# A fourth buffer of normalised tiles, absolute values moved up in ScalarE's order, and a group's moments taken over three pieces of rows

## What is computed

```python
x = x + _L0_conv_ref(_gn(x), ...)   # shifted-window attention, 7x7 windows, 8 heads
x = x + _L1_conv_ref(_gn(x), ...)   # 3x3 convolution of signs, scaled by a box sum of |x|
x = x + _L2_conv_ref(_gn(x), ...)   # 3x3 convolution with the signs of the kernel
x = x + _L3_conv_ref(_gn(x), ...)   # gated branch: causal 4-tap conv, silu, product, projection

def _gn(v, G=32, eps=1e-05):        # mean and variance over all pixels and two channels
    g = v.reshape(B_, H_, W_, G, C_ // G)
    m = jnp.mean(g, axis=(1, 2, 4), keepdims=True)
    s = jnp.var(g, axis=(1, 2, 4), keepdims=True)
    return ((g - m) / jnp.sqrt(s + eps)).reshape(v.shape)
```

## Time and profile before

| what | value |
|---|---|
| runs shown | 203.55, 207.14, 207.84 us; median 207.14 us |
| the profiled execution | 205.54 us, of which its span 203.7 us |
| mean granted TensorE clock | 0.992 |
| busy share of the span | PE 91%, DVE 76%, ACT 63%, POOL 53% |
| chain that ended last, by engine | PE 63%, DVE 21%, POOL 6%, issue 4%, ACT 3%, DMA 2% |

### The profile page before, as it was taken

How to read it: one execution, slowest core, us unless ns; L and a number is a source line. 1 busy time by engine, 2 the same in 40 slices (tenths; PEclk the granted TensorE clock), 3 DMA queues, 4 the chain that set the end, 5 groups by cost and what they waited for, 6 DMA issues and landing times.

```text
span 203.7 us, 6780 instructions
## 1 busy us (share of the span) xinstructions
PE 185.9 (91%) x2751; PEld 132.5 (65%) x2751; DVE 155.1 (76%) x318; ACT 128.3 (63%) x251; POOL 107.6 (53%) x122
## 2 busy tenths in 40 slices
PE   7967899799999997999977999999889999999994
PEld 2445887688888876879866787665446665543331
DVE  3567798978788983788983985499998768869563
ACT  2346777567957793677785567317585348789751
POOL 0349999937324049835069511936954511548470
PEclk9999999999999997999999999999999999999999
DMA  6990000000000000000000000001223540010513
GB/s 182 434 372 3 3 0 6 3 3 5 0 3 3 3 3 3 2 3 3 5 3 0 3 3 3 0 0 26 49 61 84 137 109 20 20 43 20 177 40 118
DMA packets 5021, 9.97 MB, mean 49 GB/s; under 512 B 768, under 2 KB 3840, under 8 KB 4864
## 3 DMA queue, kind: packets, MB, share of 16 engines
q1 hardware_dynamic: 4848, 9.21, 14.3%
q10 hardware_dynamic: 144, 0.34, 0.4%
HBM read 5.03 MB, written 1.61 MB: 33 GB/s over the span
## 4 chain that ended last, share of the span: by engine, by line
PE 63%; DVE 21%; POOL 6%; issue 4%; ACT 3%; DMA 2%; POOLq 0%; ACTq 0%; DVEq 0%
PE turned L831 10%; PE outs L851 10%; PE scores L952 6%; PE qkv L789 4%; PE scores L818 4%; DVE mx L1179 4%; PE turned L1034 3%; DVE d L1184 3%; PE scores L1008 3%; PE scores L968 3%; DVE st L1116 3%; PE qkv L1022 3%; PE scores L1009 3%; DMA xw<-xw_in 2%; PE outs L874 2%
## 5 line engine op out<-in xcount | busy, mean ns | idle before, releaser
L831 PE MATMUL turned<-cst,d 113*113 113x113 f32 x256 | 33.4, 274 | 4.1 <-DVE d L1184 2.9
L831 PEld LDWEIGHTS turned<-cst,d 113*113 113x113 f32 x256 | 29.4, 182 | 10.2 <-issue 5.6
L508 ACT ACTIVATE scores<-rel 113x784 f32<-113x784 f32 x32 | 25.8, 827 | 12.4 <-DVE d L1184 7.3
L213 POOL TENSOR_TENSOR kex<-ks,cst 128x784 f32<-128x784 f32 (+1 forms) x16 | 23.5, 1472 | 17.6 <-ACT ks L517 17.3
L1179 DVE TENSOR_REDUCE mx<-scores 113x16 f32<-113x784 f32 x32 | 30.8, 961 | 2.7 <-PE scores L818 2.5
L538 ACT ACTIVATE pt<-turned 113x392 f32<-113x392 f32 x64 | 28.3, 494 | 6.4 <-PE turned L831 6.3
L1184 DVE TENSOR_TENSOR d<-scores,mx 113x784 f32<-113x784 f32 x32 | 31.2, 976 | 1.1
L851 PE MATMUL outs<-vsb,pt 113*49 113x18 f32 x1024 | 29.4, 200 | 0.2 <-ACT pt L538 0.2
L851 PEld LDWEIGHTS outs<-vsb,pt 113*49 113x49 f32 x1024 | 26.4, 126 | 4.3 <-issue 0.8
L339 POOL TENSOR_TENSOR rstd<-ve,mhalf 128x1 f32<-128x1 f32 (+1 forms) x15 | 8.7, 580 | 25.8 <-DVE ve L1145 25.6
L248 POOL TENSOR_TENSOR kex<-su,sz 128x392 f32<-128x392 f32 x14 | 14.1, 1019 | 12.2 <-ACT su L662 7.1
(11 more groups left out here) (128 smaller groups left out, 373.4 us busy)
## 6 DMA issues: line engine op xcount, KB each, us to landing
p<-parts SPq DMA_DIRECT2D x14, 112.5 KB, 2.2
x<-x_in SPq DMA_DIRECT2D x1, 1568.0 KB, 10.1
out<-xw SPq DMA_DIRECT2D x8, 196.0 KB, 1.9
xs<-xs SPq DMA_DIRECT2D x8, 98.5 KB, 2.1
xw<-xw_in SPq DMA_DIRECT2D x2, 392.0 KB, 5.0
xw<-xw_in SPq DMA_DIRECT2D x1, 784.0 KB, 6.8
ker<-ker_in SPq DMA_DIRECT2D x2, 288.0 KB, 10.3
p3x<-parts SPq DMA_DIRECT2D x8, 60.0 KB, 2.0
```

Of the source, the lines that this page charges most:

```text
L213: return engine.tensor_tensor(kex[:, par, :, a * WT:b * WT], ks[:, a * WT:b * WT].rearrange("p (o t) -> p o t", o=1).broadcast_to([P, 4, n ...
L508: act.activation(o, i, ACT.Identity).then_inc(seeded, 1)
L831: mm = pe.transpose(ps_t[j][0:WK, n * WQ:n * WQ + WK], d[0:WK, k % 2, h:h + 2, :].rearrange("p a b -> p (a b)")[:, 0:WK], packed)
```

## The change

The tile xn gets a fourth buffer. POOL normalises row R+4 in turn R, behind mask_row(R+2), where it normalised row R+3 ahead of it; row 3 is normalised ahead of the loop, and rsqrt(1) moves from turn 1 to turn 0. ACT's absolutes in turns r = 3 move from the end of the turn to just behind evac_att. DVE takes the layer-1 moments of a group over image rows 3 to 16, 17 to 27 and 0 to 2 (392, 308 and 84 columns): the first piece in turn r = 0 (for the last group in turn 15), the two others and bn_aggr, over three records, where the moments stood.

```diff
-        xn = sb("xn", [P, 3, NW, WT])
+        xn = sb("xn", [P, 4, NW, WT])
...
+        sr = sb("sr", [P, 3, 6])
...
                 if R > 0:
                     pool.wait_ge(xn_ready, R)
-                if R >= 3:
-                    pool.wait_ge(v_done, R - 2)
-                pool.tensor_scalar(xn[:, R % 3].rearrange("p a t -> p (a t)"), xw[:, g, r], rstd[:, g:g + 1],
+                if R >= 4:
+                    pool.wait_ge(v_done, R - 3)
+                pool.tensor_scalar(xn[:, R % 4].rearrange("p a t -> p (a t)"), xw[:, g, r], rstd[:, g:g + 1],
                                    nmr[:, g:g + 1], ALU.mult, ALU.add).then_inc(xn_ready, 1)
...
             normalise(2)
             mask_row(1)
+            normalise(3)
             build_rel(2)
             build_rel(3)
...
-                if R == 1:
+                if R == 0:
                     rsqrt(1, 1, 2)
...
-                if R + 3 < NR:
-                    if R + 3 == NW:
-                        pool.wait_ge(ld_x1, 16)
-                    if R + 3 == 2 * NW:
-                        pool.wait_ge(ld_x2, 16)
-                    normalise(R + 3)
                 if R + 2 < NR:
                     mask_row(R + 2)
                     pool.wait_ge(kex_ready, R + 3)
+                if R + 4 < NR:
+                    if R + 4 == NW:
+                        pool.wait_ge(ld_x1, 16)
+                    if R + 4 == 2 * NW:
+                        pool.wait_ge(ld_x2, 16)
+                    normalise(R + 4)
...
                     evac_att(R - 1)
+                if R >= NW and R % NW == NW - 1:
+                    if R == 2 * NW - 1:
+                        act.wait_ge(init_pool, 3)
+                    absolutes(R // NW - 1)
                 if R + 3 < NR:
                     evac_qk(R + 3)
...
-                if R >= NW and R % NW == NW - 1:
-                    if R == 2 * NW - 1:
-                        act.wait_ge(init_pool, 3)
-                    absolutes(R // NW - 1)
...
+            def row_moments(g, n, a, b):
+
+                return dve.bn_stats(sr[:, n, :], xflat[:, g, a * HW:b * HW])
+
+            def first_moments(g):
+
+                row_moments(g, 0, SH, SH + 2 * WS)
+
+            def last_moments(g):
+
+                row_moments(g, 1, SH + 2 * WS, HW)
+                row_moments(g, 2, 0, SH).then_inc(bn_done, 1)
+                dve.wait_ge(bn_done, NG + g + 1)
+                return dve.bn_aggr(mv[:, col(1, g), :], sr[:].rearrange("p a b -> p (a b)"))
...
                     residual(R - 2)
+                if R == NR - 1 or g > 0 and r == 0:
+                    dve.wait_ge(res_done, R - 1)
+                    first_moments(g - 1 + (R == NR - 1))
...
                     dve.wait_ge(res_done, R - 1)
-                    moments(g - 1, 1).then_inc(gn_stats, 1)
+                    last_moments(g - 1).then_inc(gn_stats, 1)
...
             dve.wait_ge(res_done, NR)
-            moments(NG - 1, 1).then_inc(gn_stats, 1)
+            last_moments(NG - 1).then_inc(gn_stats, 1)
```

More of the change, by code:

```diff
@@ L786, in proj_qk @@
                     pe.wait_ge(att_ready, R - 3)
-                rhs = xn[:, R % 3]
+                rhs = xn[:, R % 4]
                 for n, name in enumerate(("wq", "wk")):
@@ L800, in proj_v @@
                     for e in range(2):
-                        mm = pe.matmul(ps_qk[64 * e:64 * e + WT, a * C:(a + 1) * C], xn[:, R % 3, a],
+                        mm = pe.matmul(ps_qk[64 * e:64 * e + WT, a * C:(a + 1) * C], xn[:, R % 4, a],
                                        ww("wv")[:, e * C:(e + 1) * C], start=True, stop=True)
```

## The result

The changed kernel takes 197.10 us (median; 196.93 to 197.21, 4 runs), the one before 205.34 us (203.46 to 207.84, 4 runs). The ratio is 0.9685, 95% interval 0.9661 to 0.9708; it compares the executions whose clock was disturbed least, so it says 3.2% where the medians say 4.0%. The profiled execution took 196.93 us with a span of 195.1 us. Forecast: 198.0 us.

The account below looks back on a forecast made before the run. PE was taken to bound the kernel, losing time in turns 8 and 12 waiting for POOL's xn and in turn 9 to the clock; 6.22 + 1.60 − 0.30 = 7.52 off 205.54 gives 198.0 us, range 195.4 to 202.6.

Parts of the forecast that it names:

- Absolutes moved up: ACT, turns 7 and 11: absolutes fit a wait ACT has anyway; row_sums then starts about 70.6 instead of 74.11.
- The cover: ACT's 1.18 us wait for PE before evac_qk(10), to hide the 1.03 us of absolutes.
- Fourth buffer: POOL, turn 7: normalise(11) done at about 66.7 to 67.2, some 9 us before PE wants it.
- the 6.22: Gain in turns 8, 9 and 12: 4.64 us from turns 8 and 12, 1.58 from turn 9 at full clock.
- the first rival: Wait passes to POOL's mask; turns 8, 9 and 12 keep their loss, only moments count: 204.2 us, chance 0.12.
- its 1.3 us of margin: mask_row(10) ends at 75.6, evac_qk(11) needs it at 76.92: margin 1.3 us.
- the 1.58: Turn 9's loss to the clock drop, 7.75 − 6.17, expected back in full; bounds 0 and 1.58.
- The rival of a drop elsewhere: One clock drop as in turn 9 behind another idle stretch: 199.6 us, chance 0.07.
- Moments in three pieces: DVE, after turns 5, 9, 13 and behind the loop: 0.40 us saved each, 1.60 in all; bounds 0.9 and 2.1.
- Price in r = 0: DVE, turns 4, 8, 12: an added bn_stats and wait for the residual cost 0.1 us each, 0.3 in all.
- First turns: POOL's earlier rsqrt(1) and moved normalise(3) delay mask_row(2) within a 5 us margin: value 0, at worst +0.5 us.
- The rule of the Trainium skill: Two-port VectorE tensor_scalar and GpSimd operations lock each other out; for signs in turns 7 and 11 nothing charged, 1.0 if met.

Follow-up runs that it names:

- e1: Kernel before with only ACT's absolutes moved up: 199.82 us against 205.32, ratio 0.9718.
- e4: Changed kernel with three buffers and POOL's old order, so absolutes up and three pieces of moments: 197.63 us, ratio 0.9617.
- e9: Kernel before with absolutes up, moments in three pieces, three buffers, and mask_row(4) ahead of normalise(5) in turn 2 alone: 196.57 us against 205.49, ratio 0.9557.
- e2: Kernel before with only the fourth buffer and POOL's new order: 201.35 us against 205.32, ratio 0.9814.
- e7: Kernel before with six matmuls of zeros in PE's idle stretch of turns 8 and 12: 203.52 us, all four runs at mean clock 1.000.
- e6: Changed kernel with the first statistics in turns r = 0 waiting for the residual before the last one: 197.00 us beside 197.10.
- e5: Kernel before with POOL's new order in turn 2 alone, mask_row(4) ahead of normalise(5): 205.78 us against 205.52, ratio 0.9934.

## Why the prediction was right, and where not

*Absolutes moved up*: right, and more than was said of it. The cover is there, ks isn't moved, and e1 gets turns 8, 9 and 12 by this edit alone.

*Fourth buffer*: the prediction gave it a share in the 6.22 without pricing it alone. Its statement that normalise(11) comes early is right; that this earns anything in turns 8 and 12 beside the moved absolutes is not (e4, e9). By itself it turns the wait for xn into a wait for the mask (e2), which is the first rival; that rival needed ab to stay late, and with ab moved its 1.3 us of margin was met to the tenth.

*The clock*: the 1.58 is right as a sum, and e7 shows its cause, PE's idleness, which the profile had only as a sequence. As a reading of turn 9 it was wrong: the prediction took 6.17 for the same work at full clock, and e7 has 6.70. The clock took 1.05 of turn 9 and 0.55 of turn 10; the other 0.53 of turn 9 was the wait for late seeds. Moving ab removes that wait, but by itself it leaves turn 10 at 7.22, not 6.68, so that turns 9 and 10 take 13.38 in e1 and in e7 alike. That the amounts came out equal was luck, as no step of the prediction had them. The doubt, why the equal stretch of turn 12 kept its clock, stays open. The rival of a drop elsewhere came true in e1, in turn 14; the changed kernel has there 0.47 us of waiting for d, e1 0.92.

*Moments in three pieces*: 0.41 saved at the pair (0.40 forecast), and 0.50, 0.46, 0.41, 0.35 in the four places. Turn 10 has its 0.46 beside a turn at a fallen clock; beside e1, whose clock was full there, it is 7.22 − 6.77 = 0.45. *Price in r = 0*: 0.22 in all where 0.3 was forecast, each time in the turn after r = 0. Turns 5, 9 and 13 take 6.28, 6.22 and 5.45 where e1 has 6.17, 6.16 and 5.40, and turns 8 and 12 take 6.23 in both. It is then given back (e6).

*First turns*: the step that failed. It put a value of 0 and no gain, because ACT and not POOL releases PE there, and looked only for a loss of up to 0.5. But DVE's small operations of turn 2, which were long beside POOL's before the change, are ahead of DVE's shift and of ACT's seeds, and POOL's new order shortened them by 0.52: 0.51 less in turn 3 (e5, e9). The rule of the Trainium skill, "SBUF — State Buffer", section "Who interferes with whom", had been weighed only for signs, where it costs nothing in the trace after either (0.62, as before); the place where it mattered was turn 2, from which the prediction quoted a row for it. The negm rows agree with the rule. In the changed kernel, however, negm is held almost as long as before (0.57), and most of the gain is ve's, another kind of instruction, which the prediction did not look at. In the kernel before ve ends at 34.61 while the sign operation beside it runs to 35.60, so there a small operation was slowed and not held for the whole of the other.

The size: 7.52 forecast, 8.60 measured, of which 0.51 is that step and 0.43 the start, which the change doesn't touch. Against the median the forecast of 198.0 was 0.9 high. It started from an execution with one clock drop in it; beside one that kept its clock (203.46) the changed kernel is 6.4 us faster.

## What to carry to other kernels

When an engine idles just before work that is late, look first for what can be moved into a wait that another engine has anyway: here 1 us of ACT's work moved into a gap of 1.2 us earned three turns. A buffer added for the same stall should be tried alone and left out alone, since what it is seen to bring may come from the order that it came with. And small operations beside long ones of GpSimd belong in the sum, with both signs.

## What was not expected of the hardware

A short idleness of PE can cost more than itself, and not always does. In the trace of the kernel before the granted clock was at 0.50 for some 3 us behind the 1.48 us of idleness in turn 8, for 1.60 us of extra time, and stayed at 1.00 behind the same idleness in turn 12. Of 37 executions 34 had a mean clock under 1.000, and filling the two stretches with six matmuls of zeros each ended this in 4 of 4 (e7). The price varies: 0.9 to 1.2 us for the drop of e1, and some 9 us at 0.50 in the profiled execution of e5, which is 0.9 us ahead of the kernel before at full clock and no faster in the median. What decides whether the clock falls, and for how long, was not tried.
